# First groups of the second mixture put ahead of and between the logits, two products that nothing reads, and gelus of the first mixture put ahead of scalings, over three pairs of PSUM banks

## What is computed

```
x = x + _L0_conv_ref(_ln_c(x), ...)       # 1x1 conv, products of channel pairs, 1x1 convs
t = _to_tokens(x)
t = t + _L0_ffn_ref(_ln_t(t), ...)        # first mixture: 2 of 8 experts for each IMAGE
x = _from_tokens(t, x)
x = x + _L1_conv_ref(_ln_c(x), L1_conv_w) # 3x3 convolution
t = _to_tokens(x)
t = t + _L1_ffn_ref(_ln_t(t), ...)        # second mixture: 2 of 8 experts for each TOKEN
```

## Time and profile before

| | |
|---|---|
| median of 3 runs | 292.63 us (291.62 to 293.29) |
| profiled execution | 289.97 us |
| its span | 288.1 us |
| mean granted PE clock | 0.988 |
| PE busy | 272.5 us, 95% |
| DVE busy | 156.7 us, 54% |
| ACT busy | 142.0 us, 49% |
| chain that ended last | PE 82%, DVE 7%, ACT 4%, waiting for nothing that shows 3% |

### The profile page before, as it was taken

One profiled execution on the slowest core, in us unless ns is written; L12 is line 12 of the kernel. 1 busy time (PEld: TensorE's weight loads), 2 busy tenths in 40 slices (PEclk: granted clock), 3 DMA queues, 4 the chain that ended last, 5 costly groups with the idle time before them and its releaser, 6 DMA issues.

```text
span 288.1 us, 6440 instructions
## 1 busy us (share of the span) xinstructions
PE 272.5 (95%) x2470; PEld 141.1 (49%) x2470; DVE 156.7 (54%) x357; ACT 142.0 (49%) x225; POOL 33.3 (12%) x74
## 2 busy tenths in 40 slices
PE   6899999999897898999999999999999999999993
PEld 4464454355664455756445534434344444444672
DVE  3676886886742285556643338484333444444444
ACT  3632333524377655045532275365665555666671
POOL 5224545300026100000000000000000000000000
PEclk9999999999999999998699999999999999999999
DMA  7726767660000000000006990000785900810010
GB/s 189 283 67 172 218 196 231 185 264 0 2 0 1 2 1 2 2 0 2 0 13 154 215 203 14 3 0 14 157 173 124 206 0 2 147 39 2 0 39 22
DMA packets 11566, 24.09 MB, mean 84 GB/s; under 512 B 2192, under 2 KB 4400, under 8 KB 11408
## 3 DMA queue, kind: packets, MB, share of 16 engines
q1 hardware_dynamic: 9808, 19.19, 27.1%
q0 software_dynamic: 1328, 3.84, 5.3%
q10 hardware_dynamic: 400, 0.66, 0.8%
HBM read 14.73 MB, written 1.33 MB: 56 GB/s over the span
## 4 chain that ended last, share of the span: by engine, by line
PE 82%; DVE 7%; ACT 4%; issue 3%; DMA 1%; DVEq 1%; ACTq 0%; POOLq 0%
PE PS L778 22%; PE PS L801 22%; PE PS L733 6%; PE PS L608 5%; PE PS L506 4%; PE PS L560 3%; PE PS L538 3%; PE PS L625 2%; PE PS L706 2%; PE PS L747 2%; PE PS L597 2%; PE PS L573 2%; PE PS L688 2%; PE PS L632 2%; DMA X<-x_in 1%
## 5 line engine op out<-in xcount | busy, mean ns | idle before, releaser
L778 PE MATMUL PS<-N,late 64*64 64x512 f32 (+1 forms) x640 | 73.1, 564 | 0.2 <-ACT h L940 0.2
L940 ACT ACTIVATE h<-PS,late 128x1024 f32<-128x1024 f32 (+1 forms) x40 | 39.2, 1024 | 34.6 <-PE PS L778 34.6
L940 ACT ACTIVATE amp<-PS,late 128x1024 f32<-128x1024 f32 (+1 forms) x40 | 39.1, 1026 | 31.8 <-PE PS L778 31.6
L778 PEld LDWEIGHTS PS<-N,late 64*64 64x64 f32 x640 | 26.7, 136 | 34.4 <-issue 33.4
L801 PE MATMUL PS<-amp,late 64*64 64x512 f32 (+1 forms) x320 | 35.5, 549 | 0.0
L801 PE MATMUL PS<-h,late 64*64 64x512 f32 (+1 forms) x320 | 35.1, 548 | 0.0
L1295 DVE SCALAR_TENSOR_TENSOR D<-PS,late,moved 128x512 f32<-128x512 f32 (+1 forms) x24 | 14.8, 657 | 28.9 <-PE PS L801 23.0
L1295 DVE SCALAR_TENSOR_TENSOR D<-PS,late,gB_odd 128x512 f32<-128x512 f32 x16 | 11.3, 747 | 28.9 <-PE PS L801 28.9
L1301 DVE TENSOR_TENSOR X<-D,X 128x512 f32<-128x512 f32 (+1 forms) x40 | 25.3, 633 | 2.1
L407 POOL DMA_DIRECT2D moved<-amp x40 | 19.7, 497 | 26.2 <-DMA moved<-amp 12.7
L842 ACT ACTIVATE Q<-PS 128x384 f32<-128x384 f32 x24 | 11.6, 488 | 21.1 <-PE PS L506 21.0
(11 more groups left out here) (151 smaller groups left out, 290.9 us busy)
## 6 DMA issues: line engine op xcount, KB each, us to landing
gB_odd<-gates_hbm SPq DMA_DIRECT2D x4, 1024.0 KB, 13.6
moved<-amp SPq DMA_DIRECT2D x40, 96.0 KB, 3.2
moved<-amp POOLq DMA_DIRECT2D x35, 96.0 KB, 2.9
moved<-gates_hbm SPq DMA_DIRECT2D x4, 512.0 KB, 7.6
moved<-gates_hbm SPq DMA_DIRECT2D x2, 1024.0 KB, 9.9
late<-late_in SPq DMA_DIRECT2D x1, 1852.0 KB, 7.5
moved<-gates_hbm SPq DMA_DIRECT2D x4, 256.0 KB, 5.3
mix<-mix_in SPq DMA_DIRECT2D x1, 897.0 KB, 9.2
```

The costliest lines, as they stand in the source:

```text
L778: mm = pe.matmul(PS[64 * r:64 * r + 64, 2 * ring(n) + half, 0:w], L("w1")[rows, u:u + 64], N[rows, a:a + w], start=True, stop=True, skip_g ...
L940: act.activation(h2[n // 2 % 2][:, 2 * (n % 2):2 * (n % 2) + 2, 0:w], pair(ring(n), w), ACT.Gelu, bias=L("b1")[:, BLOCKS * g + b:BLOCKS * ...
```

## The change

Four edits. On PE, `hidden0 4` is issued between `down0 0 0` and `down0 0 1`, ahead of the latter. On ACT, the gelu of `hidden0 5` is issued before `select_scaled 1` instead of after. `hidden0_pair` keeps three pairs of banks up to n = 9, so steps 8 and 9 take pairs 3 and 0 instead of 1 and 3, and norm 2's first `root`, which writes a bank of pair 0, waits for ten gelus instead of eight. At the second mixture's start, `warm 2` (with a wait for the first convolution's result, which had been in that bank) stands where `logits 0 0` stood; hidden 0 stands ahead of all logits, hidden 1 between the second and the third part.

```
@@ ORDER, PE
-        hidden0 0, weights, unread 5, hidden0 2, bias, down0 0 0, down0 0 1, hidden0 4, hidden0 6, down0 1 0, ...
+        hidden0 0, weights, unread 5, hidden0 2, bias, down0 0 0, hidden0 4, down0 0 1, hidden0 6, down0 1 0, ...
...
-        spread 4 0, spread 4 1, logits 0 0, spread 4 2, logits 0 1, mix 1, logits 0 2, mix 6, turn_all 0, mix 1, ...
+        spread 4 0, spread 4 1, warm 2 1, spread 4 2, mix 1, logits 0 0, logits 0 1, mix 1, logits 0 2, mix 5, turn_all 0, mix 1, ...
@@ ORDER, ACT
-        router, select 0, hidden0 0, select_scaled 0, hidden0 1, hidden0 2, hidden0 3, select 1, hidden0 4, select_scaled 1, hidden0 5, ...
+        router, select 0, hidden0 0, select_scaled 0, hidden0 1, hidden0 2, hidden0 3, select 1, hidden0 4, hidden0 5, select_scaled 1, ...
@@ hidden0_pair
-            return (0, 1, 3)[n % 3] if n < 8 else (1, 3)[n % 2]
+            return (0, 1, 3)[n % 3] if n < 10 else (1, 3)[n % 2]
@@ warm
-            def warm(n):
+            def warm(n, conv_read=0):
...
+                if conv_read:
+                    pe.wait_ge(x3_done, 1)
@@ root_
                 if i == 2:
-                    pe.wait_ge(f0_act, 4 * PAIRS // GROUPS * (b + 1))
+                    pe.wait_ge(f0_act, (10, 4 * PAIRS)[b])
```

More of the change, by code:

```diff
@@ L191 @@
         root 1 1, root 1 2, warm 2, spread 1 3, spread 1 4, unread 3, spread 1 5, warm 2, route_logits, warm 2, route_loads, warm 2, route_picks, warm 4,
-        hidden0 0, weights, unread 5, hidden0 2, bias, down0 0 0, down0 0 1, hidden0 4, hidden0 6, down0 1 0, hidden0 8, down0 1 1, hidden0 10, root 2 0, down0 2 0, hidden0 12, down0 2 1, spread 2 0, spread 2 1, hidden0 14, spread 2 2,
+        hidden0 0, weights, unread 5, hidden0 2, bias, down0 0 0, hidden0 4, down0 0 1, hidden0 6, down0 1 0, hidden0 8, down0 1 1, hidden0 10, root 2 0, down0 2 0, hidden0 12, down0 2 1, spread 2 0, spread 2 1, hidden0 14, spread 2 2,
         center 3 0, center 3 1, center 3 2, down0 3 0, down0 3 1, root 3 0, unread 3, root 2 1, spread 3 0, spread 3 1, spread 3 2, conv 0,
         spread 2 3, spread 2 4, conv 1, center 4 0, spread 2 5, center 3 3, center 4 1, center 4 2, center 3 4, root 4 0, center 3 5, unread 3, root 3 1,
-        spread 4 0, spread 4 1, logits 0 0, spread 4 2, logits 0 1, mix 1, logits 0 2, mix 6, turn_all 0, mix 1, spread 3 3, spread 3 4, mix 1,
+        spread 4 0, spread 4 1, warm 2 1, spread 4 2, mix 1, logits 0 0, logits 0 1, mix 1, logits 0 2, mix 5, turn_all 0, mix 1, spread 3 3, spread 3 4, mix 1,
         spread 3 5, mix 1, conv 2, mix 2, conv 3, mix 4, center 4 3, center 4 4, mix 2, center 4 5, mix 4, root 4 1, mix 6, spread 4 3, spread 4 4,
@@ L202 @@
         moments 1 1, moments 1 2, l1 4, l1 5, root 1 0, products 4 3, products 5 3, fc 4, fc 5, moments 1 3, moments 1 4, moments 1 5, root 1 1, root 1 2,
-        router, select 0, hidden0 0, select_scaled 0, hidden0 1, hidden0 2, hidden0 3, select 1, hidden0 4, select_scaled 1, hidden0 5, hidden0 6, hidden0 7,
+        router, select 0, hidden0 0, select_scaled 0, hidden0 1, hidden0 2, hidden0 3, select 1, hidden0 4, hidden0 5, select_scaled 1, hidden0 6, hidden0 7,
         hidden0 8, hidden0 9, moments 2 0, moments 2 1, moments 2 2, hidden0 10, hidden0 11, hidden0 12, hidden0 13, hidden0 14, hidden0 15, table 0,
```

## The result

| | before | change |
|---|---|---|
| median of 20 runs | 290.98 us | 288.28 us |
| lowest and highest | 287.28 to 293.29 | 286.88 to 289.80 |
| profiled execution | 289.97, span 288.1 | 287.14, span 285.3 |
| mean clock, profiled | 0.988 | 0.999 |

The ratio is 0.9944, 95% interval 0.9918 to 0.9969: faster, 0.56%. The medians lie 0.9% apart; the ratio is smaller because it leaves out executions more than 1.5% above the fastest of their kernel, and of the kernel before these are executions with a low clock, so a part of what the change does. The forecast was 289.4 in 288.4 to 293.1, and faster.

The account below looks back on a forecast made before the run. PE, busy 95% of the span, was taken to bound the kernel, with waits and a clock fall of some 6.9 us. 1.24 + 1.94 = 3.18, so 292.63 - 3.2 = 289.4 us, range 288.4 to 293.1.

Parts of the forecast that it names:

- Part 1: First mixture: moved steps cut waits for gelus, so norm 2's sums start 1.24 us earlier and all behind shifts; bounds 0 to 1.7.
- The 0.75 ahead of norm 2's sums: First mixture: PE, ready at 96.6, waits 0.75 us for DVE's squares before norm 2's sums start at 97.35.
- Part 2: Second mixture's start: clock stays full, gates start earlier and bind, `turn_all 0` comes 1.94 us earlier, PE waits 1.4 before it.
- the 0.86 per hidden: Second mixture's start: each hidden on PE was taken to cost 0.86 us at full clock.
- the bound was 0.65: Second mixture's start: the `warm 2` products cost at most 0.65 us against an order without them.
- rival 1: Second mixture's start: the clock did not fall there in the timed runs; 0.3 us slower, 292.9; chance 0.18.
- the 2.66 us: Whole kernel: the median of the runs shown lies 2.66 us above the profiled execution; carried over into the forecast time.
- Rivals 2 and 3: 2: clock falls anyway under hidden 0, 293.1 us, chance 0.10; 3: wait of 1.4 before `turn_all 0` brings fall, 292.8, 0.05.

Follow-up runs that it names:

- e1: The kernel before, run again unchanged; ratio 1.0015 to the other executions of it. Its profiled execution is one without the fall of the clock.
- e8: The change with its two `warm` products, but hiddens and logits at the second mixture's start in the old order; 287.4 us, ratio 0.986 to the kernel before.
- e2: The kernel before with only the first mixture's edits (order of down, hidden and gelu; three pairs of banks); 290.0 us, ratio 0.9997 to the kernel before.
- e6: The change with one hidden more ahead of the first turn of the gates and later hiddens spread differently; mean 288.5 us, ratio 0.9895 to the kernel before.

## Why the prediction was right, and where not

*Part 1, 1.24 us.* Right in its mechanism; 1.41 measured. PE's groups follow each other at 1.12 for a down and 1.17 for a hidden, I had taken 1.17 for all and a wait of 0.15 ahead of `down0 1 0` that did not come. The 0.75 ahead of norm 2's sums came as 0.72. So `hidden0 10` starts 0.18 sooner than foretold, and the sums with it. That the gain would pass through was right: 32.6 us between the sums, with and without.

*Part 2, 1.94 us against an execution with the fall.* The mechanism held, with the gates as what is late next and PE waiting 1.35 where 1.4 was foretold; the size is 1.60 at the turn of the gates (14.53 less 12.93) and 1.68 at the end. The term mis-sized is the 0.86 per hidden: where a hidden stands between logits, the next group starts 1.01 and 1.02 later (132.87 to 133.88, 135.33 to 136.35). The logits, at 1.45 for two parts and 0.77 for the third, took 0.12 more, and hidden 0 began 0.23 earlier than foretold: the products started 0.13 sooner and took 0.73 instead of 1.00 (131.57 to 132.30), the third spreads took 0.57 instead of 0.40. In sum the gates start 7.16 behind the sums of norm 3 instead of 6.89, and with 0.07 more in their chain the turn comes 0.34 late. The products cost 0.20 against an order without them, where the bound was 0.65. (A slip without effect: a clock of 0.77 from 134 to 135 puts the fall at 134.54, not at 134.46, and its length at 6.8.)

*The fall of the clock.* "The clock did not fall there in the timed runs", rival 1, had 0.18 and was set against the forecast as if one of them held for all executions. The step that failed is this either-or, and with it the 2.66 us "which no row explains; I carry it over": the kernel before falls in 62 of 99 executions and not in 32, so both hold, each for its share. Rival 1's price was 0.3 slower; by the stretches it is 0.26 faster (1.41 less 155.26 - 154.11 = 1.15), mostly since I gave the old order no wait for a gelu (0.55). With two thirds at 1.41 + 1.68 = 3.09 and one third at 0.26 the mean gain is 2.1; measured over all executions it is 290.7 - 288.4 = 2.3, by the medians of the result 2.7, and by the ratio 1.6. The forecast said 3.2 for all, twice what the ratio shows, so the gain was oversized while the time itself came out 1.1 under the forecast: the 2.66 was a trait of the three runs shown, and twenty have a median 1.0 above the profiled execution.

*The fall costs* 156.94 - 154.11 = 2.83 us of the program, not 3.4, because a full clock uncovers the wait for the gelu; between the groups of executions it is 3.6, as some have more than the one stretch (291.4 against 292.3, with e1).

*Rivals 2 and 3* show in neither profile of the change: the clock is full there while PE works, also over the wait of 1.35. Of its 32 executions none is at 0.989 or less, but five have 0.991 to 0.994, which by an estimate from the mean clock and the span is 3.4 to 5.2 us of low clock at a place that no trace shows. They take 288.9 in the mean against 288.3 of the 26 at 0.997 or more, and the two slowest of all, 289.8 and 290.3, are among them. So a fall as long as the one before is ruled out in these 32, a shorter one in a few of them is not. By the rule of the Trainium skill (TensorE: Matmul & The Clock Gate, section Why this matters for your kernels), that idle gaps lower the clock, filling 0.41 us should have changed nothing; e8 differs from e2 by the two products alone, and e2 fell in 12 of 12, e8 in none of six. The trace does not agree with that rule: no wait of PE over 0.41 us stands in the ten microseconds ahead of the fall, and one of 1.35 in the new order brought no fall. What PE did in its busy time, or that short wait, seems to have counted; no run here tells the two apart, since the products change both.

## What to carry to other kernels

One profile shows one execution: where its clock falls, look at the clocks of many before the gain is counted, and count it by shares. When steps were reordered and filled at once, try each alone: here two products, worth 0.20 us, hold the clock in the old order in six of six, and the reordering made for the same end, which alone mostly held it too, cost 0.9. A wait that is filled with a later step takes that step's cover away from where it stood (e6).

## What was unexpected of the hardware

The start scatters: the router's first product stands between 76.57 and 78.80 us in fourteen profiles, and nothing in the programs differs there. Two causes show ahead of and at PE's first `center` products. The kernel before, first execution shown, then e1:

```profile
5.55 0.88 PE L506 MATMUL PS<-X,early 128*128 128x384 f32 x2 [1.45 <-DMA X<-x_in]
6.66 0.89 PE L506 MATMUL PS<-X,early 128*128 128x384 f32 x2 [0.22 <-DMA X<-x_in]
```

```profile
5.57 1.62 PE L506 MATMUL PS<-X,early 128*128 128x384 f32 x2 [1.48 <-DMA X<-x_in]
7.40 1.62 PE L506 MATMUL PS<-X,early 128*128 128x384 f32 x2 [0.21 <-DMA X<-x_in]
```

Two instructions of 384 columns take 0.88 in the one and 1.62 in the other, which fits the lower level of the clock at the start of the kernel. Yet the stretches of e1 give it as 1.00 there:

```profile
6.00:7.00 1.00, 1.00 (x2) 0.04 (x1) 0.00 (x0) 0.00 (x0) 0.00 (x0) 1.00 1.04 235
7.00:8.00 1.00, 0.79 (x2) 0.50 (x2) 0.00 (x0) 0.77 (x2) 0.00 (x0) 1.00 1.17 308
8.00:9.00 1.00, 1.00 (x3) 0.05 (x2) 0.00 (x0) 0.10 (x1) 0.09 (x1) 1.00 1.00 247
```

The trace says why: its records of the clock begin at 9.25 us in e1, with the full level, and at 4.83 in the kernel before, and ahead of the first record the column shows 1.00 without having one. The products ahead of it are slow in both: 12 instructions of 128 columns (L514) take 2.90 from 1.20 on, where six take 0.83 at 131.92. So ahead of the first record the durations decide. Over the fourteen profiles the two go together: where the record begins at 4.1 to 4.8, the router stands at 76.57 to 76.99, where it begins at 8.5 to 11.8, at 77.54 to 78.80. The Trainium skill (TensorE: Matmul & The Clock Gate, section Part 1: The HAM clock gate) has the number of slow products at a kernel's start vary from run to run, and the trace agrees, with no slow `center` instruction in the one execution of before and four slow ones in the other. In e1 these slow products are the whole of the 1.6 us by which its router is later (78.17 against 76.57), for the first of them starts at the same time (5.57 and 5.55); in e2 it starts at 6.22, still waiting for x, so the arrival of x is the other cause. They are a reason why the mean of six runs says less than a stretch of one profile.

Second, a lower mean clock need not cost time: in e2's profile the stretch from 287 to 288, shown with e2, has 0.54, and PE has nothing to do there any more.
